# A fused attention and mixture-of-experts kernel: a third list constant, a drain on GpSimd, an earlier split of half the down weights, and row picks moved

## The reference, cut to what matters

```python
# x (8,100,512), ctx (8,722,512); then two blocks with residuals
x = x + tanh(g_xattn) * cross_attention(layernorm(x), ctx, ctx, mask)   # one 32-wide head, tiled 16 times, @ Wout + bout
# 8 experts, top 2 of a softmax over router logits, hidden 512 -> 2*1024 -> 512
z = layernorm(x)
weights, indices = top_k(softmax(z @ router_w.T), 2); weights = weights / (weights.sum(-1) + 1e-6)
h13 = einsum('bsh,ehi->bsei', z, w13); gate, up = split(h13)
y = einsum('bsei,eih->bseh', silu(gate) * up, w2)
x = x + tanh(g_ffn) * sum over the two chosen experts of weights * y
```

## Time and profile before

| | us |
|---|---|
| median of 3 runs (lowest, highest) | 417.02 (415.22, 418.81) |
| the profiled execution | 417.08 |
| its span, first to last instruction | 415.5 |
| TensorE busy in the span | 376.4 (91%) |
| VectorE, ScalarE, GpSimd busy | 220.7, 190.4, 164.2 |
| mean granted clock of TensorE | 0.965 of 2.4 GHz |

### The profile page before, as it was taken

The page is one execution under the profiler, slowest core; times in us unless marked ns, Lnnn a source line. Parts: engine busy times, 40 slices in busy tenths (PEclk is TensorE's granted clock), DMA queues, the critical chain, the costliest instruction groups (busy, mean ns, idle before and its releaser), DMA issues.

```text
span 415.5 us, 7206 instructions
## 1 busy us (share of the span) xinstructions
PE 376.4 (91%) x2046; PEld 288.1 (69%) x2047; DVE 220.7 (53%) x442; ACT 190.4 (46%) x314; POOL 164.2 (40%) x259
## 2 busy tenths in 40 slices
PE   1879999988998799998999999999999999999960
PEld 1425545576886587886878888888888888888850
DVE  2135877875728261868641256629636662962110
ACT  1123456666337242876621266438526634842120
POOL 2433678873613252333344040532424263351310
PEclk9989999995999899998999999999999999999995
DMA  7986999732099672669771148817653871210201
GB/s 258 363 292 208 341 327 325 258 105 43 26 361 416 217 267 50 207 247 346 302 248 28 22 98 287 283 34 241 236 198 79 326 261 44 41 32 0 51 0 16
DMA packets 18827, 77.75 MB, mean 187 GB/s; under 512 B 4956, under 2 KB 6108, under 8 KB 11646
## 3 DMA queue, kind: packets, MB, share of 16 engines
q1 hardware_dynamic: 11870, 66.80, 44.4%
q0 software_dynamic: 5184, 7.52, 9.4%
q10 hardware_dynamic: 1760, 3.28, 2.4%
HBM read 70.95 MB, written 7.55 MB: 189 GB/s over the span
## 4 chain that ended last, share of the span: by engine, by line
PE 62%; DMA 18%; issue 7%; POOL 6%; DVE 2%; POOLq 2%; ACT 1%; DVEq 0%
PE scp L490 14%; PE turnB L470 14%; PE turnA L470 14%; DMA out_dram<-yw,ent 7%; PE kvp L316 6%; DMA ent_next<-lists_d 6%; PE turnA L302 2%; PE kvp L477 2%; DMA xg<-xn_d,gidx 2%; POOL gidx L1080 2%; PE turnA L369 2%; POOL ent_next L1090 1%; DMA ent<-weights_d,ent 1%; PE scp L457 1%; PE turnA L353 1%
## 5 line engine op out<-in xcount | busy, mean ns | idle before, releaser
L818 DVE TENSOR_TENSOR w13l<-stage,w13h 128x1024 fp32r<-128x1024 f32 x64 | 76.0, 1219 | 5.8 <-ACT w13h L595 5.0
L595 ACT ACTIVATE w13h<-stage 128x1024 fp32r<-128x1024 f32 x64 | 65.0, 1053 | 0.0
L470 PE MATMUL turnA<-w13h,xTh 128*128 128x512 f32 x128 | 51.6, 403 | 1.7 <-DVE xTl L937 1.7
L470 PE MATMUL turnB<-w13h,xTh 128*128 128x512 f32 x128 | 52.5, 410 | 0.0
L490 PE MATMUL scp<-w2h,hTh 128*128 128x512 f32 x128 | 51.9, 405 | 0.0
L470 PE MATMUL turnB<-w13l,xTh 128*128 128x512 f32 x128 | 51.5, 402 | 0.0
L470 PE MATMUL turnB<-w13h,xTl 128*128 128x512 f32 x128 | 51.3, 401 | 0.0
L470 PE MATMUL turnA<-w13h,xTl 128*128 128x512 f32 x128 | 51.2, 400 | 0.0
L470 PE MATMUL turnA<-w13l,xTh 128*128 128x512 f32 x128 | 51.1, 400 | 0.0
L490 PE MATMUL scp<-w2h,hTl 128*128 128x512 f32 x128 | 50.4, 394 | 0.0
L490 PE MATMUL scp<-w2l,hTh 128*128 128x512 f32 x128 | 50.2, 392 | 0.0
(11 more groups left out here) (175 smaller groups left out, 643.9 us busy)
## 6 DMA issues: line engine op xcount, KB each, us to landing
stage<-in_w_dram SPq DMA_DIRECT2D x48, 1024.0 KB
ctx_t<-in_ctx_dram SPq DMA_DIRECT2D x8, 1444.0 KB
xn<-in_x_dram SPq DMA_DIRECT2D x8, 200.0 KB
xT_t<-in_xT_dram SPq DMA_DIRECT2D x8, 200.0 KB, 10.0
xn_d<-xn ACTq DMA_DIRECT2D x8, 200.0 KB
stage<-in_wout_dram SPq DMA_DIRECT2D x1, 1024.0 KB, 11.9
out_dram<-x ACTq DMA_DIRECT2D x4, 200.0 KB
out_dram<-yw ACTq DMA_DIRECT2D x2, 200.0 KB
```

The lines of the kernel that those rows point to most:

```text
L470: mm = pe.matmul(region, xp[:, c, :], wp[:, q, c, :], start=(c == 0 and i == 0), stop=(c == HC - 1 and i == 2))
L595: act.activation(dst, src, ACT.Copy).then_inc(S["w_hi"], 1)
L818: dve.tensor_tensor(lo, raw, hi.bitcast(F32), ALU.subtract).then_inc(S["w_lo"], 1)
```

## The change

The table `lists_d` gets a third column, the row to gather: it is the token number where there is an entry and 0 where the entry is empty (the memory for an empty table is now a part of `pick` and not of `kv[1]`, so the wait for its transfer moves from ScalarE's `copy_kv(1)` to VectorE's `set_pick(1)`). `gidx` and its instruction go. The read of the next list is issued before the wait for `xg_turned`, not behind it. Ahead of the loop the register loads come before the wait for the lists, and the two list reads stand together. Each iteration ends in `pool.drain()`. On ScalarE the split of unit 8 is put before y_out and waits for a new semaphore `y_half`, signalled after down 1; on VectorE the splits of units 0 to 3 are spread otherwise over the tile. In the routing, picks 4 and 6 move and `nt` is computed before the last places.

```diff
-        lists_d = nc.dram_tensor("lists_d", [ROWS, 2], I32).ap()
+        lists_d = nc.dram_tensor("lists_d", [ROWS, 3], I32).ap()
...
             outputs(NB - 1)
+            pick_rows(4, range(HC))
             ranks(NB - 1)
...
-            pick_rows(4, range(HC))
             pick_rows(5, range(HC))
+            pick_rows(6, range(HC))
             pe.wait_ge(S["nt_ready"], 1)
...
-            pick_rows(6, range(HC))
             pe.wait_ge(S["past_made"], 1)
...
+                if q == NQ // 2 - 1:
+                    mm.then_inc(S["y_half"], 1)
...
             def copy_kv(b):
-                if b == 1:
-                    act.wait_ge(S["lists_set"], 16)
...
+                    elif unit == 2 * NQ:
+                        act.wait_ge(S["y_half"], last + 1)
                     else:
                         act.wait_ge(S["y_done"], last + 2)
@@ ScalarE, tile @@
                 split(7)
+                split(8)
                 y_out(t)
-                split(8, 9)
+                split(9)
...
             def set_pick(b):
+                if b == 1:
+                    dve.wait_ge(S["lists_set"], 16)
...
+            dve.wait_ge(S["cnt_done"], 1)
+            dve.tensor_scalar(fill[:], steps_num[:], count, None, ALU.is_lt, ALU.add, accum_out=nt[:, 1:2]).then_inc(S["nt_ready"], 1)
             make_places(NB - 1)
             set_pick(NB - 1)
-            dve.wait_ge(S["cnt_done"], 1)
-            dve.tensor_scalar(fill[:], steps_num[:], count, None, ALU.is_lt, ALU.add, accum_out=nt[:, 1:2]).then_inc(S["nt_ready"], 1)
@@ VectorE, tile @@
                 h_mul(t, 0)
-                split(0, 1)
+                split(0)
                 h_mul(t, 1)
-                split(2, 3)
+                split(1, 2)
                 h_mul(t, 2)
                 h_lo(t, 0)
                 h_lo(t, 1)
-                split(4)
+                split(3, 4)
                 h_mul(t, 3)
...
-                        link(pool.tensor_copy(entry[:, :, k, 0], tok[:]))
+                        for n in (0, 2):
+                            link(pool.tensor_copy(entry[:, :, k, n], tok[:]))
...
-            def fetch(t):
-                row = pool.value_load(tile_row[0:1, bass.ds(t, 1)], min_val=0, max_val=ROWS - P)
-                pool.dma_start(ent_next[:, 0:2], lists_d[bass.ds(row, P), :]).then_inc(S["list_in"], 16)
+            def read_list(row):
+                pool.dma_start(ent_next[:, 0:3], lists_d[bass.ds(row, P), :]).then_inc(S["list_in"], 16)
+            def gather(t):
                 hold(S["list_in"], 16 * t)
-                pool.tensor_scalar(gidx[:], ent_next[:, 0:1], float(T - 1), None, ALU.min).then_inc(S["gidx_made"], 1)
-                hold(S["gidx_made"], t)
...
+            pool.wait_ge(S["tiles_ready"], 1)
+            second = row_of(1)
+            n_tiles = pool.value_load(first_tile[0:1, E:E + 1], min_val=E, max_val=TILES - 1)
             for k in range(2):
                 pool.wait_ge(S[f"lists_put{k}"], 16 * NB)
-            pool.wait_ge(S["tiles_ready"], 1)
+            read_list(second)
+            pool.dma_start(ent[:, 0:3], lists_d[0:P, :]).then_inc(S["first_in"], 16)
...
             with pool.Fori(1, n_tiles) as t:
                 entries_stay(t)
+                read_list(row_of(t + 1))
                 hold(S["xg_turned"], t + 1)
-                fetch(t + 1)
+                gather(t + 1)
+                gather_weights()
                 add_rows(t - 1)
                 entries_pass(t)
+                pool.drain()
```

More of the change, by code:

```diff
@@ L42, in gated_block @@
     NO_TOKEN = 1 << 12
+    LP = 96
     QR = D + E
@@ L45, in gated_block @@
     NSM = smalls.shape[1]
-    assert NQ * 2 * QW * 4 <= 8192 and 4 * D == P and SK % 2 == 0 and HK <= 512 and NSM == O_G + 2
+    assert NQ * 2 * QW * 4 <= 8192 and 4 * D == P and ROWS % LP == 0 and LP <= SQ and ROWS // LP * 3 <= 2 * P and SK % 2 == 0 and HK <= 512 and NSM == O_G + 2
     mask = mask.bitcast(U8).rearrange("(p n) -> p n", p=P)
@@ L94, in gated_block @@
         yw = sb(es, "yw", [P, H])
[L95 to L98, removed]
+        ent_next = sb(es, "ent_next", [P, 4], I32)
+        ent_now = sb(es, "ent_now", [P, 4], I32)
+        ent = sb(es, "ent", [P, 4], I32)
         a = ExitStack()
@@ L139, in gated_block @@
         t_num = p_num[0:E, 0:TILES]
-        empty = kv[1][:, D:D + ROWS // P * 2].bitcast(I32).rearrange("p (r t) -> p r t", t=2)
+        empty = pick[0:LP, 1:3, :].rearrange("p b n -> p (b n)")[:, 0:ROWS // LP * 3].bitcast(I32).rearrange("p (r t) -> p r t", t=3)
         half = sb(a, "half", [SQ, 3])
@@ L164, in gated_block @@
         place = sb(a, "place", [SQ, NB, 2], I32)
-        entry = sb(a, "entry", [SQ, NB, 2, 2], I32)
+        entry = sb(a, "entry", [SQ, NB, 2, 3], I32)
         nt = sb(a, "nt", [E, 3])
@@ L196, in gated_block @@
         names2 = """st13_0 st13_1 st13_2 st13_3 st2_0 st2_1
-        w_hi w_lo gu_done silu_done h_done ht_done hh_done hl_done y_done y_ready
-        list_in first_in gidx_made weight_in gathered yw_free ent_kept ent_copied y_added xg_turned xh_done xl_done""".split()
+        w_hi w_lo gu_done silu_done h_done ht_done hh_done hl_done y_half y_done y_ready
+        list_in first_in weight_in gathered yw_free ent_kept ent_copied y_added xg_turned xh_done xl_done""".split()
         S.update({n: sem(n) for n in names2})
@@ L262, in _ @@
             sp.wait_ge(S["empty_made"], 1)
-            sp.dma_start(lists_d.rearrange("(p r) t -> p r t", p=P), empty).then_inc(S["lists_set"], 16)
+            sp.dma_start(lists_d.rearrange("(p r) t -> p r t", p=LP), empty).then_inc(S["lists_set"], 16)
             for b in range(3, NB):
@@ L654, in y_out @@
                 act.wait_ge(S["yw_free"], t + 1)
-                act.activation(yw[:], scp[:, 512:512 + H], ACT.Copy, scale=ent[:, 2:3].bitcast(F32)
+                act.activation(yw[:], scp[:, 512:512 + H], ACT.Copy, scale=ent[:, 3:4].bitcast(F32)
                                ).then_inc(S["y_ready"], 1)
@@ L1073, in hold, with row_of, gather_weights @@
                 pool.sem_inc(S["pool_held"], 1)
-            def fetch(t):
-                row = pool.value_load(tile_row[0:1, bass.ds(t, 1)], min_val=0, max_val=ROWS - P)
-                pool.dma_start(ent_next[:, 0:2], lists_d[bass.ds(row, P), :]).then_inc(S["list_in"], 16)
-                hold(S["list_in"], 16 * t)
-                pool.tensor_scalar(gidx[:], ent_next[:, 0:1], float(T - 1), None, ALU.min).then_inc(S["gidx_made"], 1)
-                hold(S["gidx_made"], t)
-                if isinstance(t, int):
-                    pool.wait_ge(S["xn2_put"], 16 * NB)
-                pool.indirect_dma_start(xg[:], None, xn2_d, bass.IndirectOffsetOnAxis(gidx[:], 0)).then_inc(S["gathered"], 16)
-                if isinstance(t, int):
-                    pool.wait_ge(S["weights_put"], 16)
-                fetch_weights(ent_next)
-            def fetch_weights(to):
-                pool.indirect_dma_start(to[:, 2:3], None, weights_d, bass.IndirectOffsetOnAxis(to[:, 1:2], 0)).then_inc(S["weight_in"], 16)
+            def read_list(row):
+                pool.dma_start(ent_next[:, 0:3], lists_d[bass.ds(row, P), :]).then_inc(S["list_in"], 16)
+            def row_of(t):
+                return pool.value_load(tile_row[0:1, bass.ds(t, 1)], min_val=0, max_val=ROWS - P)
+            def gather(t):
+                hold(S["list_in"], 16 * t)
+                pool.indirect_dma_start(xg[:], None, xn2_d, bass.IndirectOffsetOnAxis(ent_next[:, 2:3], 0)).then_inc(S["gathered"], 16)
+            def gather_weights():
+                pool.indirect_dma_start(ent_next[:, 3:4], None, weights_d, bass.IndirectOffsetOnAxis(ent_next[:, 1:2], 0)
+                                        ).then_inc(S["weight_in"], 16)
             def entries_stay(t):
```

9 lines of the change are left out of this document (5 added, 4 removed).

## The result

The changed kernel takes **398.82 us** (median of 4 executions, 397.32 to 399.13), the kernel before 417.16 beside it (415.22 to 418.81): a ratio of 0.9555, with a 95% interval of 0.9507 to 0.9603. Forecast were 404.7 and a range of 402.5 to 410.5. The direction was right, the time was not. The profiled execution took 399.05, its span is 397.5 against 415.5, the mean granted clock 0.980 against 0.965.

A forecast was written before the change was run, and what follows sets the result against it. Bound by attention and routing to 100 us, GpSimd's loop to 216.80, then TensorE alone. From 417.08, 1.9 (routing) + 7.0 (tiles 1 to 3) + 3.2 (lone tile) + 0.8 (tile 5) - 0.5 = 12.4 gives 404.7 us; range 402.5 to 410.5.

The forecast's parts named there:

- The drain: End of each GpSimd loop iteration: costs between 0 and 0.57 us, taken as 0.2, with nothing left to wait for.
- slower: the drain: Rival, GpSimd's loop: the drain holds each iteration; from 3.6 us the gain is lost, at 4.6 some 426; chance 0.03.
- Routing, 1.9: End of the routing on TensorE: moved picks start the last pick sooner, perhaps at full clock; 1.9 us, ends 1.3 and 2.4.
- So does its start at half clock: Start of tile 0 on TensorE: the 1.75 idle before it remains, and its first products still run at half clock.
- the pick ahead of the ranks: Routing on TensorE: a pick put in the idle 1.30 before the ranks costs 0.95 and delays nothing.
- GpSimd's prelude and loop, tiles 1 to 3: GpSimd before and in its loop: loop starts 7.6 us sooner, each iteration 0.8 shorter; tiles 1 to 3 win 7.0.
- the second rival: GpSimd's loop: transfers, not instructions, keep it at 19.3 us; only some 2 us won, 415; chance 0.08.
- 1.2 late by the plain count: GpSimd five gathers on, formerly at 216.80: reaches 205.0 while TensorE would ask at 203.8; what is left priced at 0.5.
- The first rival: GpSimd's first gathers: the stall moves from `gidx` into the gather, waiting for VectorE's w2 splits; 408.7 us, chance 0.20.
- The lone tile: Tile 4, expert 2's only tile: the new order of splits wins 3.2 of 3.7 us, bounds 2.5 and 3.7.
- Tile 5 on: Tiles from 5 to the last output: 0.8 us won, less 0.5 for what GpSimd leaves.
- better than forecast: Case at tile 0 and routing: clock back before tile 0, saving 1.6, with the routing's full 2.4; 402.3 us, chance 0.05.

The follow-up runs named there:

- changed_again: The changed kernel run once more, unaltered, as partner of other runs on the same chip: 399.19 us, ratio 0.9592 to the kernel before.
- late_list: The changed kernel with the read of the next list put behind the wait for `xg_turned` again: 399.98 us, ratio 0.9594 to the kernel before.
- old_picks: The changed kernel with the picks and `nt` in their old order: 398.87 us, ratio 0.9579 to the kernel before.
- half_drained: The changed kernel with its loop split: iterations 1 to 7 with the drain, 8 to 15 without; 407.59 us in one execution (kernel before 419.52).

## Why the prediction was wrong

**The step that failed: "The drain: no row shows one. From below it is 0 ... I take 0.2, as nothing is left to wait for."** A gain from the drain was excluded with a reason that spoke only of the output's transfers, and the only place looked at was the loop. With it went an unwritten term: the working has no line for what lies behind y_out 15, so its 13.6 us were taken as fixed. The runs put 6.3 us there (13.15 without a drain, 6.88 with one), which by itself is more than the 5.9 by which 404.7 missed 398.82. That there was something at the end could be read from the trace of the kernel before: 7.5 us with no engine and no DMA busy. That a drain takes it away could not. With these 7.5 us as the drain's bound, and not 0, the range would have reached down to 397. As for "nothing is left to wait for" in the loop, the drain costs 0.4 an iteration and 2.15 in the first, where 0.2 was taken; that is far below the 3.6 that the rival "slower: the drain" needed.

**Routing, 1.9: right up to tile 0, too large behind it.** From the ranks to the first product it was 9.18 before and 7.21 after, and the last pick took 1.13 instead of 2.08, at full clock. But tile 0 took 120.04 - 99.23 = 20.81 instead of 19.60. "So does its start at half clock" took tile 0's share of the half clock as fixed; six profiles with the moved picks have 19.39 to 20.81 there. And the pick ahead of the ranks doesn't fit into their idle 1.30: with what is left of the wait it takes 1.05 + 0.42 = 1.47. That is 0.2 of the 1.1 by which the ranks stood later in this execution. In the mean of the profiles 28.8 - 27.4 - 0.2 = 1.2 is left of the 1.9; the medians don't show it.

**GpSimd's prelude and loop, tiles 1 to 3: right in size (7.2 for 7.0, no stop of TensorE), in part by luck.** The loop began at 113.47 for 114.5, with errors that cancel. The first list read stood 4.10 for the landing of the last scatter, a wait that the sum left out, and began at 101.98 and not 99.8. The gather took 2.93, more than its 1.1 to 2.2, and tile 0's weights were issued at 110.65 and not 108.0. On the other side their landing, kept at 5.87, came within 2.8 (110.65 to 113.47). Before, the DMA engines were at 0.98 from 116 to 122, beside it; after, they were at 0.02 from 111 to 112, so the rows suggest, without an experiment on it, that these weights now come ahead of the 1 MB loads.

The loop itself hardly became shorter: 207.40 - 113.47 = 93.9 for five iterations, 18.8 each against 19.3 before, where 0.8 less was forecast; in `changed_again` it is 19.6. To that extent the second rival, that transfers and not instructions set the loop, is true, and what keeps TensorE running is the lead that the prelude gives. It is used up near tile 5: in `changed_again` TensorE stood 1.21 for a gather at 206.24, the place and the size of the prediction's own "1.2 late by the plain count". In `late_list` one gather was 3.5 late, in tile 2.

The first rival came true in its cause and not in its effect. The gather beside VectorE's w2 splits, in `old_picks` and in the kernel after:

```profile
102.87 7.28 POOL L1089 DMA_INDIRECT xg<-xn_d,ent_next  x1 [1.79 <-DMA ent_next<-lists_d]
104.76 4.49 DVE L823 TENSOR_TENSOR w2l<-stage,w2h 128x2048 fp32r<-128x2048 f32 x2
...
103.68 4.49 DVE L823 TENSOR_TENSOR w2l<-stage,w2h 128x2048 fp32r<-128x2048 f32 x2
```

The first gather ends 0.9 behind the last w2 split in all 11 profiles of kernels without `gidx`, wherever it began: after 1.54 in `changed_again`, 2.93 here (106.14 to 109.07, the splits to 108.17), 7.28 in `old_picks` (102.87 to 110.15, the splits to 109.25), 8.15 in `half_drained`. The second gather took 1.00. VectorE's two splits took 4.49 in each of the 11. In `old_picks` the gather began beside the w13 splits ahead of them (100.22 to 104.85) and waited for those of w2 as well. The Trainium skill ("SBUF — State Buffer", Who interferes with whom) says that a VectorE instruction with two SBUF inputs and a GpSimd instruction that reads SBUF contend; the gather's row numbers lie in SBUF. The trace agrees; at this place it is always GpSimd that waits, and for the whole row of splits and not for one of them. So the wait only moved from `gidx` to the gather. It had no effect because the loop still began 8.6 sooner.

**The lone tile: right** in size (3.3 for 3.2) and in its condition: the splits alone win nothing in the kernel before and 2.9 us in the changed one. The second h comes 0.18 late; no wait of ScalarE for unit 8's load shows, which was priced at 0.

**Tile 5 on: 1.1** for 0.3 net; in this execution GpSimd left nothing over, where 0.5 had been set aside; in `changed_again` it left the 1.21 told above.

With the tail's term and without the routing's, the prediction's own sum would have been 417.08 - (7.0 + 3.2 + 0.8 - 0.5) - 6.3 = 400.3; with 1.2 for the routing it is 399.1. One slip in it changes nothing: "better than forecast" comes by its own terms to 404.7 - 1.6 - 0.5 = 402.6, not 402.3.

## What to carry to other kernels

Split the whole span into pieces, the one behind the last computed output too, and ask for the busy times of each: a stretch in which nothing is busy is a term of the sum like any other. Where GpSimd runs a loop with transfers and such a stretch stands at the end, try one drain at a place where GpSimd waits anyway, late in the kernel; here a drain was worth 1.5% alone. An improvement on an engine that is second on the path shows nothing until the first is mended (the splits: 0 alone, 2.9 together), so time parts both alone and taken out of the whole. A reading of where the clock falls and comes back needs several profiles of the same code: one pair of them can show a cost that the next pair doesn't.

## What the runs showed of the hardware

GpSimd leaves something undone that isn't in any engine's or DMA's rows and that the program's end waits for: 0.31 to 0.34 us for each iteration of this loop, 1.3 for what came ahead of it, 0.06 for one more small indirect transfer. A drain takes it from the end and costs GpSimd time of the same size where it stands: 1.8 ahead of the loop, 2.15 after the first iteration where none stood ahead, 0.4 for each later one. What it is, the runs don't tell.

A gather on GpSimd that meets VectorE's splits (two inputs in SBUF) ends 0.9 us behind the last of them, in 11 profiles of 11, whether it takes 1.54 or 8.15 for that; alone it takes 1.0.

TensorE's clock fell near 93 and was back near 103 with the old order of the picks; with the moved ones it fell in the idle time ahead of tile 0 or right behind it, between 96.8 and 99.7, and was back between 101.5 and 105.2. The same code had 6 to 13 long products at half clock.
